# Expert weights loaded from the last attention chunk, and row slots freed by a copy of the tokens' weights

## The reference, cut to what matters

```python
topk_idx, topk_w = _route(x, router_w, e_bias)             # 8 of 64 experts for each token
coef = jnp.zeros((T, E), topk_w.dtype).at[jnp.arange(T)[:, None], topk_idx].add(topk_w)
g = jnp.einsum('th,ehi->tei', x, Wg)
u = jnp.einsum('th,ehi->tei', x, Wu)
h = jax.nn.silu(g) * u * coef[:, :, None]
moe_out = jnp.einsum('tei,eih->th', h, Wd)
shared = jax.nn.silu(x @ SWg) * (x @ SWu) @ SWd
return (moe_out + shared).reshape(orig_shape)
```

## Time and profile before

| | |
|---|---|
| median of 3 runs | 3275.7 us |
| profiled execution, own time | 3276.76 us |
| its span in the trace | 3274.9 us |
| TensorE busy | 2773.5 us (85%) |
| VectorE busy | 2721.3 us (83%) |
| ScalarE busy | 1943.8 us (59%) |
| GpSimd busy | 953.5 us (29%) |
| moved by DMA | 264.55 MB |

### The profile page before, as it was taken

How to read it: one execution, slowest core, us unless ns; L and a number is a source line. 1 busy time by engine, 2 the same in 40 slices (tenths; PEclk the granted TensorE clock), 3 DMA queues, 4 the chain that set the end, 5 groups by cost and what they waited for, 6 DMA issues and landing times. The chain is left out here.

```text
span 3274.9 us, 132532 instructions
## 1 busy us (share of the span) xinstructions
PE 2773.5 (85%) x55642; PEld 2460.6 (75%) x55642; DVE 2721.3 (83%) x6827; ACT 1943.8 (59%) x5180; POOL 953.5 (29%) x928
## 2 busy tenths in 40 slices
PE   3888888888888888888888888888886199999986
PEld 3878888887787888788788888888786177777664
DVE  2889898888989988999999999999997156777776
ACT  2656555556666655666666555666654077666664
POOL 3112222222222222223222222233221101444444
PEclk8988898888888988989999899999998599999998
DMA  3321111111111111111111111111110945777776
GB/s 116 82 64 37 36 35 35 35 35 37 39 35 35 37 37 35 43 35 35 39 40 41 35 35 35 35 42 35 39 40 30 347 144 170 221 217 224 220 217 180
DMA packets 209563, 264.55 MB, mean 81 GB/s; under 512 B 30673, under 2 KB 183250, under 8 KB 208210
## 3 DMA queue, kind: packets, MB, share of 16 engines
q1 hardware_dynamic: 183936, 188.53, 19.0%
q0 software_dynamic: 24576, 67.27, 7.2%
q10 hardware_dynamic: 466, 0.27, 0.0%
HBM read 125.37 MB, written 130.58 MB: 78 GB/s over the span
## 5 line engine op out<-in xcount | busy, mean ns | idle before, releaser
L379 POOL DMA_INDIRECT table<-tail,places x256 | 277.1, 1082 | 721.1 <-DVE BR L852 214.8
L1496 PE MATMUL bank<-w,tail 128*128 x1280 | 357.2, 401 | 31.4 <-ACT tail L1539 14.5
L1468 POOL DMA_INDIRECT tail<-y_table,places x256 | 249.5, 975 | 449.3 <-DMA y_table<-tail 314.0
L1091 POOL COPY inv_r<-N 32x512 f32<-32x512 f32 x128 | 136.4, 1065 | 734.0 <-DVE N L827 730.0
L445 DVE TENSOR_TENSOR tri<-tri,step 128x58 f32<-128x58 f32 (+13 forms) x896 | 305.5, 341 | 30.8
L444 DVE TENSOR_TENSOR step<-tri 128x58 f32<-128x58 f32 (+13 forms) x896 | 301.4, 336 | 26.4
L1496 PEld LDWEIGHTS bank<-w,tail 128*128 128x128 f32 x1280 | 219.2, 191 | 95.9 <-issue 72.7
L1586 DVE TENSOR_TENSOR more<-tail 128x1 f32<-128x1 f32 x320 | 50.8, 159 | 193.7 <-ACT tail L1548 189.6
L1511 PE MATMUL bank<-w,tail 128*128 x640 | 191.1, 380 | 2.7 <-DVE tail L1597 1.4
L1546 ACT ACTIVATE tail<-bank 128x129 f32<-128x129 f32 x320 | 89.8, 281 | 158.9 <-PE bank L1496 156.3
L1482 PE MATMUL bank<-ident,tail 128*128 128x128 f32 x640 | 125.1, 278 | 66.1 <-DMA tail<-table 65.6
(11 more groups left out here) (275 smaller groups left out, 8103.8 us busy)
## 6 DMA issues: line engine op xcount, KB each, us to landing
table<-blank SPq DMA_DIRECT2D x320, 128.5 KB, 3.2
tail<-table SPq DMA_DIRECT2D x320, 128.5 KB
y_table<-tail SPq DMA_DIRECT2D x320, 128.0 KB
w<-in_wpack_dram SPq DMA_DIRECT2D x16, 1540.0 KB, 19.3
tail<-in_x_dram SPq DMA_DIRECT2D x66, 64.0 KB, 2.5
x_rows<-tail SPq DMA_DIRECT2D x32, 128.0 KB
sh_rows<-tail SPq DMA_DIRECT2D x32, 128.0 KB, 1.9
table<-tail,places POOLq DMA_INDIRECT x256, 2.9
```

The lines of the kernel that those rows point to most:

```text
L379: nc.gpsimd.indirect_dma_start(out=table, out_offset=bass.IndirectOffsetOnAxis(ap=t.places[:, TOP * (n - 1) + k:TOP * (n - 1) + k + 1], ax ...
L1468: nc.gpsimd.indirect_dma_start(out=t.term[2 * (m % 2) + k], out_offset=None, in_=d.y_table[0:P * closed(b) + P + 1, :], in_offset=bass.Ind ...
L1496: mm = nc.tensor.matmul(ps[:, 0:257], t.xT_slot[i % 3][:, P * kt:P * kt + P], weights(i, 257 * kt, 257), start=(kt == 0), stop=(kt == 1))
```

## The change

`w` is allocated first, and the attention's tensors are carved out of it (`alloc_attention` now takes pieces of `t.w`, with `wq`, `wk`, `wa`, `war`, `wv`, `z`, `k` and `q` in front). The experts 0 to 17 lie over these eight tensors, the experts 62 and 63 over the end of the region, which no tensor of the attention reaches. In the last chunk SyncE waits until the last product that reads `wv` and the last reader of `z`, `k` and `q` are done, and issues six loads with 20 experts, in front of its wait for `x2_made`. In `last_tile` it issues 11 loads instead of 16. In `experts`, VectorE copies the rows' 257th number into `share` three steps ahead of `hidden`, and SyncE's load of the rows of tile s waits for the transposes of tile s-6 and for that copy, and no more for `h_ready`.

```diff
+EARLY = [(0, 4), (4, 8), (8, 12), (12, 16), (16, 18), (62, 64)]
+
+
+def load_experts(eng, t, d, begin, end, sem):
+    eng.dma_start(t.w[:, begin:end, :], d.wpack[begin:end].rearrange("e p k -> p e k")).then_inc(t.sem[sem], 16)
...
-def alloc_attention(nc, ctx, t):
+def alloc_attention(t):
+
+    take = carve(t.w[:, :, :].rearrange("p e k -> p (e k)"), E * PACK)
...
+                if n == chunks - 1:
+                    wait_done(sp, t, o, n - 1, "V1")
+                    sp.wait_ge(t.sem["queries_made"], o.base("queries_made", n))
+                    for begin, end in EARLY:
+                        load_experts(sp, t, d, begin, end, "w_early")
                 sp.wait_ge(t.sem["x2_made"], n + 1)
...
+            sp.wait_ge(t.sem["w_early"], 16 * len(EARLY))
...
-            for e in range(0, E, 4):
-                sp.dma_start(t.w[:, e:e + 4, :], d.wpack[e:e + 4].rearrange("e p k -> p e k")).then_inc(t.sem["w_loaded"], 16)
+            for e in range(18, 62, 4):
+                load_experts(sp, t, d, e, e + 4, "w_loaded")
...
                     if s >= X_RING:
-                        sp.wait_ge(t.sem["h_ready"], s - X_RING + 1)
+                        sp.wait_ge(t.sem["xT_done"], s - X_RING + 1)
+                        sp.wait_ge(t.sem["share_taken"], s - X_RING + 1)
...
             def hidden(i):
                 dve.wait_ge(t.sem["sig_ready"], i + 1)
-                dve.wait_ge(t.sem[f"row_loaded{i % X_RING}"], 16 * (i // X_RING + 1))
-                x, sig, h, ps = t.x_slot[i % X_RING], t.sig_slot[i % 3], t.h_slot[i % 3], t.ps[gu_bank[i % 3]]
-                nc.vector.tensor_tensor(t.share[:, i % 8:i % 8 + 1], sig[:, 0:1], x[:, 256:257], ALU.mult)
+                dve.wait_ge(t.sem["share_taken"], i + 1)
+                sig, h, ps = t.sig_slot[i % 3], t.h_slot[i % 3], t.ps[gu_bank[i % 3]]
+                nc.vector.tensor_tensor(t.share[:, i % 8:i % 8 + 1], sig[:, 0:1], t.share[:, i % 8:i % 8 + 1], ALU.mult)
...
+            def take_share(i):
+                dve.wait_ge(t.sem[f"row_loaded{i % X_RING}"], 16 * (i // X_RING + 1))
+                nc.vector.tensor_copy(t.share[:, i % 8:i % 8 + 1], t.x_slot[i % X_RING][:, 256:257]).then_inc(
+                    t.sem["share_taken"], 1)
...
+            for i in range(3):
+                take_share(i)
             for s in range(last):
+                if s + 3 < TILES:
+                    take_share(s + 3)
                 if s < TILES:
                     hidden(s)
```

More of the change, by code:

```diff
@@ L21 @@
 import collections
+import math
 from contextlib import ExitStack
@@ L170, in alloc_shared @@
              "sh_sig_ready", "sh_h_ready", "tab_stored", "tab_loaded", "tab_ready", "blank0_stored", "blank1_stored", "blank2_stored",
-             "w_loaded", "xT_done", "gu_done", "hT_done", "y_done", "xT_ready", "sig_ready", "h_ready", "hT_ready", "y_ready",
-             "sig_link", "h_link", "y_stored0", "y_stored1", "y_stored2", "gathered0", "gathered1", "pair_added",
+             "w_loaded", "w_early", "xT_done", "gu_done", "hT_done", "y_done", "xT_ready", "sig_ready", "h_ready", "hT_ready", "y_ready",
+             "share_taken", "sig_link", "h_link", "y_stored0", "y_stored1", "y_stored2", "gathered0", "gathered1", "pair_added",
              "sh_loaded0", "sh_loaded1", "x2_loaded", "fin_link", "fin_var", "fin_guess", "fin_done", "out_stored0", "out_stored1"]
@@ L206, in alloc_tail @@
     t.tile_of, t.page_order = take(3), take(3)
-def alloc_attention(nc, ctx, t):
+def alloc_attention(t):
+    take = carve(t.w[:, :, :].rearrange("p e k -> p (e k)"), E * PACK)
     def sb(name, shape):
-        return ctx.enter_context(nc.sbuf_tensor(name, shape, F32))
+        ap = take(math.prod(shape[1:]))
+        if len(shape) == 3:
+            return ap.rearrange("p (a b) -> p a b", b=shape[2])
+        if len(shape) == 4:
+            return ap.rearrange("p (a b c) -> p a b c", b=shape[2], c=shape[3])
+        return ap
     t.wq, t.wk, t.wa, t.war = (sb(n, [P, 2, 1024]) for n in ("wq", "wk", "wa", "war"))
     t.wv = sb("wv", [P, 2, 2, 512])
+    t.z = sb("z", [P, 2, 1024])
+    t.k, t.q = sb("k", [P, 16, C]), sb("q", [P, 16, C])
     t.wo = sb("wo", [P, 8, 256])
@@ L224, in alloc_attention @@
     t.pq_mask = sb("pq_mask", [P, 2, C])
-    t.restart = ctx.enter_context(nc.sbuf_tensor("restart", [P, 1024], mybir.dt.bfloat16))
+    t.restart = sb("restart", [P, 512]).bitcast(mybir.dt.bfloat16)
     t.ones_pair = sb("ones_pair", [P, P])
@@ L233, in alloc_attention @@
     t.xnT = sb("xnT", [P, 2, P])
-    t.z = sb("z", [P, 2, 1024])
     t.c = sb("c", [P, 2, 16, C])
@@ L237, in alloc_attention @@
     t.dec_end = [sb(f"dec_end{i}", [P, 2, 16]) for i in range(2)]
-    t.k, t.q = sb("k", [P, 16, C]), sb("q", [P, 16, C])
     t.kplus_both = sb("kplus", [P, 2, 1024])
@@ L1517, in _ @@
                 if s == 2:
-                    pe.wait_ge(t.sem["w_loaded"], 16 * (E // 4))
+                    pe.wait_ge(t.sem["w_loaded"], 16 * 11)
                 if 2 <= s <= TILES + 1:
@@ L1677, in program @@
         alloc_tail(nc, whole, t)
[L1678 to L1691, removed]
-        alloc_weights(nc, whole, t)
+        alloc_weights(nc, whole, t)
+        alloc_attention(t)
+        consts = [(t.lnw[:], a["lnw"]), (t.lnb[:], a["lnb"]), (t.ident[:], a["ident"]), (t.wa[:], a["wa"]),
+                  (t.gate_bias[:], a["gate_bias"]), (t.war[:], a["war"]), (t.wk[:], a["wk"]), (t.wq[:], a["wq"]),
+                  (t.bg_bias[:], a["bg_bias"])]
+        late = [(t.wv[:], a["wv"]), (t.wo[:], a["wo"]), (t.wbg[:], a["wbg"]),
+                (t.eye[:], a["eye"]), (t.neg_strict[:], a["neg_strict"]), (t.ones_pair[:], a["ones_pair"]),
+                (t.pq_mask[:], a["pq_mask"]), (t.rw[:], a["rw"]), (t.e_bias[:], a["e_bias"]), (t.shg[:], a["shg"]),
+                (t.shu[:], a["shu"]), (t.shd[:], a["shd"]), (t.upper[:], a["upper"]),
+                (t.blank[:], a["blank"]), (t.tile_of[:], a["tile_of"])]
+        first_front(nc, t, X, d, consts, late)
+        clear(nc, t.sems)
+        attention(nc, t, chunks, X, d)
+        clear(nc, t.sems)
         alloc_experts(t)
```

## The result

The changed kernel takes 3244.49 us (median of 6 executions, 3230.55 to 3249.88), the kernel before, on the same chip, 3269.63 us (6 executions). The ratio is 0.9908, with an interval of 0.9887 to 0.9929: by the ratio 30 us faster (23 to 37), by the two medians 25 us, where 15 were forecast. Against the forecast of 3260.4 us it is 16 us less; 6 of these come from the kernel before, whose median over six executions lies under the 3275.7 us of the first three. The profiled execution is the fastest of the six (3230.55 us). The two profiles stand 46 us apart, 16 us more than the change brings by the ratio.

The account below looks back on a forecast made before the run. Bounds: VectorE in the attention, then the weights' transfer, then a 15.8 us loop per 8 tiles through a late row load. Profiled 3276.76 - 19.8 + 4.5 = 3261.5, median 1.1 lower: 3260.4 us, range 3256.7 to 3269.3; 8 in 10: 3241 to 3272.

Parts of the forecast that it names:

- The weights: Wait for experts' weights behind the attention: loading 20 of 64 experts early saves 19.8 us, at most 21.2.
- the 5 to 14 forecast: Last attention chunk: six early issues delay SyncE's x2 store by some 5 to 14 us, costed at nothing.
- SyncE was to stay the last at the barrier: Barrier of `last_tile`: SyncE would arrive at about 2577.0 us, still behind ScalarE's 2574.4.
- Layout and first tiles: Attention's tensors over `w` change addresses only: nothing; tiles before the gathers, whose slots come free earlier, also nothing.
- The copies: VectorE's 320 added copies: two per block paid at 0.08 us over 28 blocks, 4.5 us; bounds 2.2 to 13.4.
- nothing while the row is waited for by TensorE anyway: VectorE's new wait for row s+3 before `hidden(s)`: no cost, since TensorE would feel a late row first.
- The row slots: Row loads freed of the wait for h: most leave about 1 us earlier, the late one doesn't; no gain.
- So I take no gain there: Late row load in each block: it lands no sooner although the load ahead left 1 us earlier; gain 0.
- the late row: Row load numbered a multiple of 8, queued behind y store, output stores and x2 load; TensorE stalls for it.
- rival 1: Tiles with gathers: earlier row loads remove stalls, 28 x 0.44 = 12.3 us, giving 3248 us (3232 to 3254); chance 0.25.
- row load 160: Evidence against sooner landing: its predecessor left 3.56 us ahead, yet it took 3.75 us against 3.79 for load 200.
- Rivals 2 and 3: 2: early weights half paid by longer last chunk, 3270 us, chance 0.09. 3: gathers later in blocks, 3297 us, 0.08.

Follow-up runs that it names:

- b2: The kernel before the change, unaltered, run again under a second name on chip B: ratio 1.0006, 3291.9 us.
- a2: The whole change, unaltered, run again on chip B against the kernel before: ratio 0.9982, 3284.5 us.
- b3: The kernel before the change, unaltered, run again on chip D: ratio 1.0005, 3263.9 us.
- e11: Early weights and new layout only, no copies, row loads wait for h as before; against the kernel before, chip D: ratio 0.9926, 3237.3 us.
- e10: Kernel before with only the attention's tensors moved over the weights, no early weights or copies; chip D: ratio 1.0005, 3263.8 us.
- e3: The changed kernel, copies included, but row loads also wait for h as before; against the kernel before, chip A: ratio 0.9971, 3298.9 us.
- e1: Early weights and new layout only, no copies, row loads wait for h as before; against the kernel before, chip A: ratio 0.9932, 3290.8 us.
- e13: The changed kernel, copies included, but row loads also wait for h as before; against the kernel before, chip E: ratio 0.9969, 3250.9 us.
- a4: The whole change, unaltered, run again on chip E against the kernel before: ratio 0.9920, 3236.0 us.
- e7: The changed kernel with the copy made on ScalarE instead of VectorE, slots still freed; ratio to the kernel before, chip C: 0.9910, 3244.1 us.
- e2: Freed row slots with copies and new layout, all 16 weight loads in `last_tile`; against the kernel before, chip A: ratio 1.0036, 3318.6 us.
- e12: Freed row slots with copies and new layout, no early weights; against the kernel before, chip D: ratio 0.9973, 3253.4 us.
- e5: The changed kernel, but row loads wait for h except tiles 7 modulo 8; ratio to the kernel before, chip B: 0.9954, 3272.9 us.
- e6: The changed kernel, but row loads of tiles 7 modulo 8 also wait for h; ratio to the kernel before, chip B: 0.9968, 3280.8 us.

## Why the prediction was right or wrong

**The weights: right.** 19.8 us were forecast. The stretch became 20.3 us shorter from before to the change (75.6 to 55.3 us from the attention's end to the first transpose), and 20.4 and 18.5 us in pairs on one chip (b2 75.3, a2 54.9; b3 74.6, e11 56.1). The time fell by 24 us, with an interval that holds 20. The last chunk cost nothing, and the x2 store came 5.8 us later, at the lower end of the 5 to 14 forecast. One detail was wrong: SyncE was to stay the last at the barrier. ScalarE now comes 1.6 us behind it, with no cost that shows.

**Layout and first tiles: right.** e10 has 1.0005, and the steps ahead of the gathers take 1.80 us.

**The attention, 12 us shorter in the first pair of profiles** (2537.1 to 2525.2), is no effect of the change. It ended at 2537, 2522 (b2) and 2515 us (b3) in three traces of the kernel before, and at 2539 us with the layout alone. It is scatter between executions, and the larger part of the 16 us by which the two profiles exaggerate the change. It goes with the clock that TensorE was granted: up to the attention's end the mean is 0.900 of full speed in the first trace and 0.901 in e10 (2539 us), but 0.910 in the changed kernel and 0.912 in b3. The prediction calls the attention bound by VectorE; VectorE was busy there for 2238 us in all four within 3 us, so its work alone doesn't set the length.

**The copies: right in sign, size uncertain.** 4.5 us were forecast, with bounds of 2.2 and 13.4. With the wait for h kept, the times differ by 8 us by the medians or 13 by the ratios (e3 against e1), and 11 or 14 us (e13 against e11, on two chips of one kind). By the granted clocks given under the last heading, some 7 us of each pair may be the clock's, as an estimate, so 4.5 isn't refuted. All copies of the changed kernel, one group:

```profile
L1617 DVE COPY more<-tail x320: 120/144/155, 2580.5 to 3194.7; 128x1 f32<-128x1 f32 x160
```

The Trainium skill, in "VectorE: DVE Perf Modes", section "The TRN2 errata", gives a measured fixed term of about 150 cycles for an instruction, as an estimate 0.16 us. The trace roughly agrees for the duration, with 0.144 us, and not for the distance: in the timeline of a4 the next operation starts 0.08 us behind a copy (2966.26 and 2966.34 us). The term most open to doubt is the wait. The prediction said "nothing while the row is waited for by TensorE anyway"; in e13 the copy held VectorE up for 18.8 us, and behind it stand `hidden`, `weigh` and the y store, behind which the next row load stands. That this wait, and not more copies on the path than two a block, makes the cost is argued and not shown; in e7, with freed slots, taking both away gained nothing that shows.

**The row slots: wrong.** The step that failed is "So I take no gain there". It put the gain of the freed slots at 0; the release measured 15 us on chip E (a4 against e13). The issue of the late row did stay, 2.2 us behind the end of `weigh` (2.3 before, medians), and four of the other seven did leave 0.45 us behind it; both were forecast. But the row landed 0.30 us sooner by its last packet and was used 0.43 us sooner by the means above, as rival 1 has it, whose mechanism is that the load ahead has left earlier and makes room. The argument against it was a single transfer, row load 160 with 3.75 us. Such loads took between 3.0 and 5.6 us in the chain of waits of the changed kernel, so one of them says nothing; the mean over all late rows, with the distance to the load ahead, was the thing to ask for. Rival 1 priced it at 12.3 us, with 0.44 us a block. With the measured 0.30 us it is, as an estimate, 28 x 0.30 = 8.4 us; what makes up the rest of the 15 us, beyond the copies' shorter wait, isn't shown.

**The sum.** The forecast had -19.8 + 4.5 + 0 = -15. The runs have -24 for the weights and -9 for slots and copies together (release -15; +8 to +14 for the copies as measured with the wait kept), and -30 for the whole. Rival 1 (3248 us, a chance of 0.25) is the case that happened. That its time came out within 4 us is in part luck: the base fell by 6 us, and the parts measured differ from its terms. Rivals 2 and 3 didn't: the weights pay in full, and VectorE's wait for gathers is 11.0 us where over 20 was the mark.

The Trainium skill has the rule beside rival 1, in "DMA: Bandwidth & Descriptors", section "Rules for kernel authors": issue a DMA early and wait for it late. The runs on D and E agree, with 9 us (the copies' cost taken off) and 15 us; e2 on A doesn't.

**What stays open.** That the release brings a gain on chips of the first kind is shown by e12 on D (9 us with the copies' cost taken off) and by a4 against e13 on E (15 us); which of the earlier transfers makes room for the late row is not. e5 and e6 ran on chip B, where the late row sets little of the pace, and put part of it on the load directly ahead and part on the others. And on A and B the freed slots with their copies cost 12 us (e2) and some 17 us (a2, against the weights' share of chip A, as an estimate); why wasn't found, though of the 12 us of e2 some 9 go with a lower granted clock, by the estimate at the end.

No version is clearly faster than the change: e7, 0.9910, is level with it, and e5 on chip B, 12 us under it by the medians, had the higher mean clock (0.9152 against 0.9116).

## What to carry to other kernels

A load that leaves at the same moment can still land sooner when its neighbours leave earlier, so "its issue stays" doesn't mean "no gain", and one transfer is no evidence against it: average over all repeats of the pattern. Where the landing can be read from packets, take it rather than the time of use, which also holds what the reader itself was late by. An instruction that is moved ahead brings its wait with it; cost the wait and what is queued behind it, not only the instruction. And compare the granted clock of two versions before a few us between them are called a cost.

## What was not expected of the hardware

The same program runs in two ways on different chips. The kernel before takes 3261.5 to 3275.3 us on C, D and E and 3293.3 to 3308.1 us on A and B; its stretch is 451.6 us (first profile) and 448.4 us (b3), but 488.3 us on B (b2). The difference lies mostly in the step of TensorE to the tiles whose number leaves 4 when divided by 8: on average 3.1 to 3.8 us in the eight traces of A and B, and 1.8 to 2.0 us in the traces of the other chips, with waits that no operation of the trace explains. The slots alone changed sign with it: 0.9973 on D, 1.0036 on A. And the attention, which no edit of e10 or b3 alters but in its addresses, ended 24 us apart in these two traces of one chip.

Much of the scatter goes with TensorE's granted clock. Its mean over an execution lay between 0.903 and 0.919. In the 277 executions of the five groups, each compared with the mean of its own series (one kernel on one chip), 0.01 more goes with 25 us less (correlation -0.80); over the 20 traces the attention's end and the clock up to it have a correlation of -0.90. The two kinds of chip are hardly told apart by it: the kernel before has a mean of 0.909 on A and 0.912 on B, and 0.911 on C and 0.913 on D and E. But pairs of versions are: e3 has 0.9104 and e1 0.9130, e13 0.9129 and e11 0.9158, e2 0.9058 and the kernel before 0.9094 on chip A. At 25 us for 0.01, as an estimate, that is 7 us of the 12 and 13 between the means of the first two pairs and 9 of the 12 in the third; e12 and e10 have the same clock (0.9113, 0.9114), so the 10 us between them stand. Whether the clock is the cause there or follows from something in these versions isn't shown.
